# A quantised decoder layer on one Trainium2 core: two running maxima instead of three, joined exponent factors, token halves, and more unread TensorE products

## What is computed

```python
# block 1: fq_* scale by a power of two from the global absolute maximum, round to 8 bits
h    = layer_norm(x) * fq_round(gamma) + fq_round(beta)
qkv  = fq_floor(fq_floor(h) @ fq_round(w_qkv))          # 16 heads of 64
dots = fq_floor(einsum(q, k) * temp)
attn = fq_floor(softmax(dots))
x1   = layer_norm(x + fq_floor(fq_floor(attn @ v) @ fq_round(w_out)))
# block 2: linear cross attention with a 8x8 matrix for each of 16 heads
x2   = layer_norm(x1 + layer_norm(q(x1) @ (k(ctx).T @ v(ctx)) * scale + x1))
# block 3: both products on affine 8-bit codes from the global min and max
out  = layer_norm(x2 + qlinear(gelu(qlinear(x2, W1, b1)), W2, b2))
```

## Time and profile before

| | |
|---|---|
| median of 3 runs | 462.2 us (461.14 to 462.81) |
| profiled execution, its own time | 462.34 us |
| its span, first to last instruction | 460.6 us |
| busy share of the span: DVE, ACT, PE, PEld, POOL | 88%, 75%, 58%, 27%, 31% |
| mean granted TensorE clock | 0.732 of full speed |
| HBM traffic | 7.75 MB read, 1.58 MB written |

### The profile page before, as it was taken

The page is one execution under the profiler, slowest core; times in us unless marked ns, Lnnn a source line. Parts: engine busy times, 40 slices in busy tenths (PEclk is TensorE's granted clock), DMA queues, the critical chain, the costliest instruction groups (busy, mean ns, idle before and its releaser), DMA issues.

```text
span 460.6 us, 7277 instructions
## 1 busy us (share of the span) xinstructions
PE 267.8 (58%) x1800; PEld 126.0 (27%) x1807; DVE 406.2 (88%) x1293; ACT 345.9 (75%) x789; POOL 144.8 (31%) x321
## 2 busy tenths in 40 slices
PE   5688986876677733333323333179997767164371
PEld 3564432332222210000000000033343655051260
DVE  5868998879699999999999999858977986987977
ACT  2599966788999946999999999926676845537233
POOL 2400000001000001999999999970000004530010
PEclk9989997989655555555555555569999997679596
DMA  7600000000444421799899998790002200000002
GB/s 269 160 1 1 1 0 1 24 23 24 176 165 179 186 110 50 161 202 200 200 201 201 204 208 183 137 212 18 1 0 73 85 1 0 1 0 1 0 1 92
DMA packets 84249, 43.24 MB, mean 94 GB/s; under 512 B 69095, under 2 KB 74487, under 8 KB 84090
## 3 DMA queue, kind: packets, MB, share of 16 engines
q1 hardware_dynamic: 82650, 42.69, 36.6%
q10 hardware_dynamic: 1568, 0.21, 0.3%
HBM read 7.75 MB, written 1.58 MB: 20 GB/s over the span
## 4 chain that ended last, share of the span: by engine, by line
DVE 36%; ACT 27%; PE 19%; issue 15%; ACTq 2%; DMA 1%; DVEq 0%; SPq 0%
ACT mem L968 20%; PE ps L471 18%; DVE mem L1090 6%; DVE mem L1250 4%; DVE d_max L1093 4%; DVE mem L1513 3%; DVE m L1650 2%; ACT mem L902 2%; DVE m L1651 2%; ACT mem L938 1%; ACTq L968 1%; DMA mem<-in_x 1%; DVE c L1089 1%; DVE mem L1301 1%; DVE mem L1520 1%
## 5 line engine op out<-in xcount | busy, mean ns | idle before, releaser
L471 PE MATMUL ps<-mem 64*128 64x256 bf16 (+5 forms) x1182 | 179.2, 352 | 113.9 <-DVE row_max L1342 80.0
L968 ACT ACTIVATE mem<-mem,neg_max 128x256 f32<-128x256 int16 x256 | 125.8, 494 | 9.2 <-DVE neg_max L1089 9.2
L471 PEld LDWEIGHTS ps<-mem 64*128 64x128 bf16 (+3 forms) x1188 | 66.2, 118 | 219.0 <-DVE row_max L1342 108.5
L1342 DVE CUSTOM_DVE_ANT_0 mem<-ps,fold,c 128x256 int16<-128x256 f32 x256 | 110.8, 470 | 0.2 <-DVE fold L1090 0.2
L429 POOL TENSOR_SCALAR mem<-mem,r_now 128x256 int16<-128x256 f32 x176 | 81.4, 482 | 76.9 <-DVE r_now L1089 76.8
L471 PE MATMUL ps<-minus,ones_bf 128*128 128x256 bf16 x266 | 38.6, 314 | 32.5 <-DVE m L1651 9.8
L1250 DVE TENSOR_TENSOR mem<-mem 128x1024 bf16<-128x1024 bf16 x76 | 49.7, 685 | 6.3 <-ACT mem L902 3.7
L918 ACT ACTIVATE mem<-ps,c 128x1024 bf16<-128x1024 f32 x48 | 48.3, 1296 | 1.6 <-PE ps L471 1.6
L968 ACT ACTIVATION_READ_ACCUMULATOR mem<-mem,neg_max x256 | 48.3, 189 | 0.0
L938 ACT ACTIVATE mem<-ps,c 128x1024 int16<-128x1024 f32 x32 | 36.2, 1209 | 11.6 <-DVEq L1285 6.2
L471 PEld LDWEIGHTS ps<-minus,ones_bf 128*128 128x128 bf16 x266 | 29.6, 113 | 40.7 <-DVE m L1651 10.2
(11 more groups left out here) (205 smaller groups left out, 358.6 us busy)
## 6 DMA issues: line engine op xcount, KB each, us to landing
...
```

Of the source, the lines that this page charges most:

```text
L471: return te.matmul(o_, l_, r_, start=start, stop=stop)
L968: ins = sc.activation(e_ring[:, u % 4, pos], y_ring[:, u % 4, pos], ACT.Exp, scale=scale_reg, bias=neg_max[:, u % 4, pos:pos + 1], accum_o ...
L1342: ins = ve.tensor_tensor_reduce(y_ring[:, slot, pos], ps[:, 2 * slot + pos // 2, (pos % 2) * N:(pos % 2 + 1) * N], shift, col("g_dots"), - ...
```

## The change

It does the following.

- `max_pass`: two running maxima instead of three. A fold now waits for the fold two back, not three back. After the loop they are joined; then halves of 512 columns are folded onto each other, for the running maximum and for the last unit, so that the last reduction reads 512 columns. The direct maxima (`md`) go onto the diagonal by themselves, and the rest is joined into the diagonal in `across_bf`.
- `scale_of` can give the codes' factor itself: numerators (`numerator`) are made ahead of time. Floors of the dots' shift (`f_qt`) are made in `temperature`, four linked operations there instead of a maximum and a reciprocal after the crossing.
- Behind the attention's product: one maximum over 1024 columns instead of two over 512, joined by the diagonal.
- x2's first rounding moves from DVE to ACT (two halves); both copies of the transposed x2 are DVE's. The hidden units come in the order of `HID_UNITS`; the codes of the hidden layer are made in two halves of tokens, and the second product of a half starts when its four codes are there. `zero_point` comes after the first part of it.
- PE: transposes and products of the cross attention alternate by quarter. `keep_clock` counts change (24 to 36, 24 to 26, 60 to 78, 22 to 32, 40 to 26), new ones are put in (22 before the crossing of the QKV maximum, 18 before the attention's product, 8 after the first transpose of x1), and one product stands ahead of each unit of the QKV code pass but the first three and units 9, 11, 21 and 24. The crossing of the QKV maximum comes ahead of `kv_main(0)` and `kv_bias(0)`.

In the diff, eight leading blanks and unchanged lines are left out; the number is the line before.

```diff
@@ -124 @@
-run_max = at(168, [3, UNIT], BF16)
+run_max = at(168, [2, UNIT], BF16)
@@ -188 @@
+ident_g = diag[:, 1]
@@ -253 @@
+HID_UNITS = [(2 * k + j, h) for k in range(HC // 2) for h in range(2) for j in range(2)]
@@ -459 @@
-    pl.tensor_scalar(hid_i[:, 2], hid[:, 2], col("inv"), 0.0, ALU.mult, ALU.add)\
-        .then_inc(sem("hid_i_pool"), 1)
+    for h in range(2):
+        cols = slice(h * UNIT, (h + 1) * UNIT)
+        pl.tensor_scalar(hid_i[:, 2, cols], hid[:, 2, cols], col("inv"), 0.0, ALU.mult, ALU.add)\
+            .then_inc(sem("hid_i_pool"), 1)
@@ -510 @@
-    keep_clock(24, 6)
+    keep_clock(36, 6)
@@ -633 @@
+            if n >= QKV_RING and n not in (9, 11, 21, 24):
+                keep_clock(1, 2 * (u % QKV_RING))
...
+                keep_clock(22, 6)
+                across_bf(7)
...
-                across_bf(7)
@@ -695 @@
-    keep_clock(24, 1)
+    keep_clock(26, 1)
...
+    keep_clock(18, 1)
@@ -751 @@
-    keep_clock(60, 5)
+    keep_clock(78, 5)
@@ -773 @@
-    for q in range(3):
+    transpose_x1(0)
+    keep_clock(8, 5)
+    for q in range(1, 4):
...
-    for q in range(3):
-        cross_attention(q)
-    transpose_x1(3)
+        cross_attention(q - 1)
@@ -791 @@
-    for u in range(2 * HC):
-        hc, h = u // 2, u % 2
-        if u < 2:
-            pe.wait_ge(sem("x2T_act" if h else "x2T_dve"), 1)
+    for u, (hc, h) in enumerate(HID_UNITS):
+        pe.wait_ge(sem("x2T"), h + 1)
...
-    pe.wait_ge(sem("x2_m"), 10)
-    keep_clock(22, 2)
+    pe.wait_ge(sem("gelu_done"), 2 * HC)
+    pe.wait_ge(sem("x2_m"), 9)
+    keep_clock(32, 2)
...
-    keep_clock(40, 2)
-    pe.wait_ge(sem("hid_codes"), HC)
+    keep_clock(26, 2)
...
+        pe.wait_ge(sem("hid_codes"), HC * (1 + t // 8))
@@ -899 @@
-                sc.activation(run_max[:, nth] if nth < 3 else abs_t[:, nth % 3],
+                sc.activation(run_max[:, nth] if nth < 2 else abs_t[:, nth % 3],
@@ -915 @@
-                sc.activation(run_max[:, k] if first and k < 3 else abs_t[:, k % 3],
+                sc.activation(run_max[:, k] if first and k < 2 else abs_t[:, k % 3],
@@ -981 @@
-            act.wait_ge(sem("o_last"), 2)
+            act.wait_ge(sem("o_last"), 1)
@@ -1052 @@
-    act.wait_ge(sem("x2T_ps"), 2)
-    sc.activation(x2T[:, UNIT:], ps[:, 7].bitcast(BF16), ACT.Copy).then_inc(sem("x2T_act"), 1)
+    act.wait_ge(sem("x2_inv"), 1)
+    for h in range(2):
+        sc.activation(x2_i[:, 8 * h:8 * h + 8], x2[:, 8 * h:8 * h + 8], ACT.Copy,
+                      scale=col("inv")).then_inc(sem("x2_i"), 1)
...
-    for u in range(2 * HC):
-        hc, h = u // 2, u % 2
+    for u, (hc, h) in enumerate(HID_UNITS):
@@ -1064 @@
-    for hc in (1, 3):
-        sc.activation(hid_i[:, hc], hid[:, hc], ACT.Copy, scale=col("inv")).then_inc(sem("hid_i_act"), 1)
+    for h in range(2):
+        for hc in (1, 3):
+            cols = slice(h * UNIT, (h + 1) * UNIT)
+            sc.activation(hid_i[:, hc, cols], hid[:, hc, cols], ACT.Copy, scale=col("inv"))\
+                .then_inc(sem("hid_i_act"), 1)
@@ -1104 @@
-    def across_bf(bank):
-        ts(diag_b[:, 0], ident_b[:], col("m"), None, ALU.mult).then_inc(sem("diagonals"), 1)
+    def across_bf(bank, value, spread):
+        ve.scalar_tensor_tensor(diag_b[:, 0], spread, value, diag_b[:, 0], ALU.mult, ALU.max)\
+            .then_inc(sem("diagonals"), 1)
@@ -1119 @@
-    def scale_of(grown, n, s_out, inv_out, factor=HALF_RANGE, done=None):
+    def scale_of(grown, n, s_out, inv_out, factor=HALF_RANGE, over=float(0x7F000000), done=None):
...
-        ins = ts(inv_out.bitcast(I32), bits, -1.0, float(0x7F000000), ALU.mult, ALU.add)
+        ins = ts(inv_out.bitcast(I32), bits, -1.0, over, ALU.mult, ALU.add)
...
+    def numerator(name):
+        ts(col("n_" + name), col(name).bitcast(I32), float(0x3F800000), None, ALU.add)
+        return ts(col("k_" + name), col(name), HALF_RANGE, None, ALU.mult)
@@ -1205 @@
-    ts(col("k_hw"), col("s_hw"), HALF_RANGE, None, ALU.mult)
+    numerator("s_hw")
@@ -1218 @@
+        link(ts(col("s_qt"), col("s_qq"), col("temp"), None, ALU.mult))
+        link(ts(col("f_qt"), col("s_qt"), 1.0e-30, None, ALU.max))
+        link(ve.reciprocal(col("f_qt"), col("f_qt")))
+        link(ts(col("f_qt"), col("f_qt"), FLOOR, None, ALU.mult))
@@ -1225 @@
-        dve.sem_inc(sem(f"{phase}_folded"), 6)
+        dve.sem_inc(sem(f"{phase}_folded"), 5)
@@ -1243 @@
-                k = nth % 3
-                if 3 <= nth < total - 1:
+                if 2 <= nth < total - 1:
+                    run = run_max[:, nth % 2]
...
-                    dve.wait_ge(sem(f"{phase}_folded"), nth + 1)
-                    ve.tensor_tensor(run_max[:, k], run_max[:, k], abs_t[:, k], ALU.max)\
+                    dve.wait_ge(sem(f"{phase}_folded"), nth + 2)
+                    ve.tensor_tensor(run, run, abs_t[:, nth % 3], ALU.max)\
...
-        k = (total - 1) % 3
-        others = [j for j in range(3) if j != k]
+        half = UNIT // 2
+        run, last = run_max[:, 0], abs_t[:, (total - 1) % 3]
...
-        for j in others:
-            link(ve.tensor_tensor(run_max[:, k], run_max[:, k], run_max[:, j], ALU.max))
+        link(ve.tensor_tensor(run, run, run_max[:, 1], ALU.max))
...
-        link(ts(cb[:, 0:1], col("md"), grow, None, ALU.mult))
+        link(ve.tensor_tensor(run[:, 0:half], run[:, 0:half], run[:, half:], ALU.max))
+        link(ts(diag_b[:, 0], ident_b[:], col("md"), grow, ALU.mult, ALU.mult))
...
-        link(ve.tensor_tensor(run_max[:, k], run_max[:, k], abs_t[:, k], ALU.max))
-        link(ve.tensor_reduce(col("m"), run_max[:, k], AX.X, ALU.max))
-        link(ts(col("m"), cb[:, 0:1], col("m"), None, ALU.max))
+        link(ve.tensor_tensor(last[:, 0:half], last[:, 0:half], last[:, half:], ALU.max))
+        link(ve.tensor_tensor(run[:, 0:half], run[:, 0:half], last[:, 0:half], ALU.max))
+        link(ve.tensor_reduce(col("m"), run[:, 0:half], AX.X, ALU.max))
...
-    across_bf(7)
-    scale_of(col("x"), 1, col("s_qkv"), col("i_qkv"), factor=col("k_hw"))
-    ts(col("g_qkv"), col("s_hw"), col("i_qkv"), None, ALU.mult).then_inc(sem("qkv_scale"), 1)
+    across_bf(7, col("m"), ident_b[:])
+    scale_of(col("x"), 1, col("s_qkv"), col("g_qkv"), factor=col("k_s_hw"), over=col("n_s_hw"), done="qkv_scale")
...
-    dve.wait_ge(sem("qkv_scale"), 1)
@@ -1321 @@
-    across_bf(7)
+    across_bf(7, col("m"), ident_b[:])
...
-    link(ts(col("g_dots"), col("s_qq"), col("temp"), col("i_dots"), ALU.mult, ALU.mult))
+    link(ts(col("g_dots"), col("i_dots"), col("s_qt"), None, ALU.mult))
...
-    dve.wait_ge(sem("dots_scale"), 1)
-    link(ts(col("shift"), col("g_dots"), 1.0e-30, None, ALU.max))
-    link(ve.reciprocal(col("shift"), col("shift")))
...
-        ins = ts(shift[:, k * P:(k + 1) * P], ones[:], col("shift"), FLOOR, ALU.mult, ALU.mult)
+        ins = ts(shift[:, k * P:(k + 1) * P], ones[:], col("f_qt"), col("s_dots"), ALU.mult, ALU.mult)
@@ -1396 @@
-    scale_of(col("x"), 1, col("s_attn"), col("i_attn"))
-    ts(col("g_fine"), col("i_attn"), 1.0 / FINE, None, ALU.mult).then_inc(sem("attn_scale"), 1)
+    scale_of(col("x"), 1, col("s_attn"), col("g_fine"), over=float(0x7F000000 - (14 << 23)), done="attn_scale")
...
-    ts(col("k_av"), col("s_av"), HALF_RANGE, None, ALU.mult)
-    dve.wait_ge(sem("attn_scale"), 1)
+    numerator("s_av")
@@ -1429 @@
+        if grp == 21:
+            link(ts(ident_g, ident[:], GROW, None, ALU.mult))
@@ -1458 @@
+    link(ts(diag_b[:, 0], ident_b[:], col("m"), None, ALU.mult))
...
-    for k in range(2):
-        dve.wait_ge(sem("av_group"), B * GROUPS - 1 + k)
-        absmax(d_max[:, k:k + 1], ps[:, last_bank + k, :]).then_inc(sem("o_last"), 1)
-    dve.wait_ge(sem("o_last"), 2)
-    link(ts(cb[:, 0:1], d_max[:, 0:1], d_max[:, 1:2], GROW, ALU.max, ALU.mult))
-    link(ts(col("m"), cb[:, 0:1], col("m"), None, ALU.max))
-    across_bf(6)
-    scale_of(col("x"), 1, col("s_o"), col("i_o"), factor=col("k_av"))
-    ts(col("g_o"), col("s_av"), col("i_o"), None, ALU.mult).then_inc(sem("o_scale"), 1)
+    dve.wait_ge(sem("av_group"), B * GROUPS)
+    absmax(d_max[:, 0:1], ps[:, last_bank:last_bank + 2].rearrange("p a n -> p (a n)"))\
+        .then_inc(sem("o_last"), 1)
+    dve.wait_ge(sem("o_last"), 1)
+    across_bf(6, d_max[:, 0:1], ident_g)
+    scale_of(col("x"), 1, col("s_o"), col("g_o"), factor=col("k_s_av"), over=col("n_s_av"), done="o_scale")
...
-    ts(col("k_ow"), col("s_ow"), HALF_RANGE, None, ALU.mult)
-    dve.wait_ge(sem("o_scale"), 1)
+    link(numerator("s_ow"))
@@ -1496 @@
-    scale_of(col("x"), 1, col("s_proj"), col("i_proj"), factor=col("k_ow"))
-    ts(col("g_proj"), col("s_ow"), col("i_proj"), None, ALU.mult).then_inc(sem("proj_scale"), 1)
-    dve.wait_ge(sem("proj_scale"), 1)
+    scale_of(col("x"), 1, col("s_proj"), col("g_proj"), factor=col("k_s_ow"), over=col("n_s_ow"), done="proj_scale")
@@ -1629 @@
+    def zero_point():
@@ -1637 @@
+    zero_point()
...
```

(38 more changed lines are left out.)

## The result

The changed kernel takes 454.3 us in the median of four runs (453.64 to 456.63), the kernel before 461.7 us beside it (460.41 to 462.81): ratio 0.9853, 95% interval 0.9824 to 0.9882. The profiled execution takes 454.38 us by its own time, 8.0 less than the one of before; its span is 452.7 us, its mean granted clock 0.749 (0.732 before). The forecast was 452.3 us: 454.3 lies just above its own range (449.5 to 454) and inside the one with the rivals (449.3 to 456.2).

What follows compares the result with a forecast made beforehand. The prediction took the chain of waits to be mostly ACT and DVE, with TensorE on it where its clock is low. Terms summing to 10.05 us off 462.3 gave 452.3 us, own range 449.5 to 454, with rivals 449.3 to 456.2.

Steps and rivals of the forecast that it cites:

- the second rival: POOL takes more of the layer norm's gain and of the hidden codes': 454.3 us, chance 0.14.
- step 1: Join of the maxima, done twice: narrower folds and reduction gain 0.8 us a time, between 0 and 1.6.
- step 9: Start of the kernel: 12 more products may hold the clock over a pause, -0.2 us.
- step 2: QKV code pass: start -0.2, its slow pieces -0.7, half clock -1.3, single products +0.2; -2.0 us, bounds -0.2 and -3.0.
- step 3: Dots: join 0.8, maximum and reciprocal gone behind the crossing 0.4; -1.2 us, bounds -0.4 and -2.0.
- steps 4 and 5: Attention product without half-clock steps, -2.2 us; scale of the product and of the projection, -0.65 us.
- step 6: Layer norm 1 and cross attention: first product and statistics earlier, less POOL contention; -1.7 us, bounds -0.6 and -2.7.
- step 7: Codes of x2: ACT rounds both halves, no longer copies transposed x2, Gelu earlier; -1.2 us, bounds -0.6 and -1.4.
- step 8: Codes of the hidden layer: made in halves, `output(0)` starts at once; -0.9 us, bounds +0.3 and -1.5.
- The first: Rival: the clock still falls in the QKV code pass, 2.0 us lost and about 1.5 more; 455.8 us, chance 0.18.
- The third: Rival: the clock falls between crossing and attention product, 2.2 us lost, up to 1.7 of delay; 456.2 us, chance 0.10.
- the fourth and the fifth: Rivals: added products hold the clock nowhere, 457.5 us, chance 0.04; whole code pass at half clock, 468 us, chance 0.04.

Runs made afterwards that it cites:

- the best version: Changed kernel without code-pass single products, POOL's second hidden half-unit on ACT, 26 products behind x2's crossing, products ahead of code units 3 to 5: 452.4 us, ratio 0.9794.
- the second trace of before: The kernel before, unchanged, run once more for another trace: 462.8 us, one run.

## Why the prediction was right, and where it was not

Direction and cause of most of the gain were right. Four stretches brought 2.3 us less than forecast, three 0.24 more. The sum of 452.3 us missed by 2.0; that 454.3 is also what the second rival had in time is chance, since only a part of the miss was POOL's.

**Join (step 1).** Right: 0.76 against 0.8 a time, shown by putting it back.

**Start (step 9), 0.2 forecast, 0.20 measured.** This is not shown to be a gain: eleven traces with the same instructions up to there reach the last maximum at 64.42 to 64.97 us, and the two of before at 64.71 and 64.46.

**QKV code pass (step 2), 2.0 forecast, 1.07 measured.** The forecast was 0.2 for the start, 0.7 for its slow pieces, 1.3 for the fall at 101 us, less 0.2 for the single products. Set against the best version's trace, which has no single products and full clock throughout, the terms measure 0.02, 0.51 (first to fourth unit 8.16 us before, 7.65 there), 1.44 and, for the products, 0.85. So three things failed. DVE's start gained nothing: from the last maximum to its first unit it is 8.98 us before and 8.96 after, since what `temperature` and the longer diagonal add takes up all that join and factor save. "Two of them show, +0.2" put the products' cost at a quarter: PE is the chain in more places than at `xm_half` (38.96 us against 38.11, both at full clock). Its premise, a DVE step of 2.2 us throughout, was read from the last units only; in the changed kernel seven of the fifteen steps are longer than 2.4 us. And "in the 5.18 us piece half clock costs 1.3" was right as a size in that trace (6.24 us against 4.80 for the two steps of DVE) but no effect of the change: it was one execution's, since the second trace of before lacks it, and so does the changed kernel without any products. That the products hold the clock in this pass is not shown by any run.

**Dots (step 3), 1.2 forecast, 0.77 measured.** The exponentials' first row maxima came 1.12 us earlier against the last maximum, as forecast; 0.35 was lost again just ahead of the row sums' minimum, where DVE idles before an operation of 128x8:

```profile
300.26 0.20 DVE L1369 RECIPROCAL row_inv<-row_sums 128x8 f32<-128x8 f32 x1 [3.37 <-ACT mem L975]
300.92 0.17 DVE L1101 TENSOR_SCALAR r_now<-row_inv 128x8 f32<-128x8 f32 x1 [0.46 <-DVE row_inv L1369]
```

Before, the second starts 0.31 us behind the first. The run with the old join has 0.31 too, with the same instructions there, and so has the second trace of before; all eleven traces with the new join have 0.66. So it is no matter of one execution. Of the 0.77 us that the new join saves at the dots about 0.3 reach this minimum (138.59 us with the old join, 138.26 here). What the idle time is stays open.

**Attention product and scales (steps 4 and 5), 2.85 forecast, 2.95 measured.** Right in sum, with luck in it: taking the products away gives back 1.4, not 2.2, and the second trace of before is 0.8 quicker in this stretch than the first, by which the gain would be 2.2. So my steps at half clock were counted rightly, but from a trace that had more of them.

**Cross attention (step 6), 1.7 forecast, 1.84 measured.** The sum was right and its reason wrong. I gave the gain to the order and called the 78 products a means to it. The runs gave 0.1 to the order, since DVE's wait for POOL takes back what it saves, and 1.7 to the products and with them the clock. Both halves of that had stood in the prediction: three transposes at half clock, and up to two shifts losing 0.5.

**Codes of x2 (step 7), 1.2 forecast, 0.67 measured.** The term of the first unit was mis-sized: in this execution the clock fell as the hidden layer's first products began (0.83 in 409 to 410 us, 0.50 after), and Gelu waited 0.43 us for them. In the traces where the clock is up the stretch takes 7.34 to 7.36 us, which would be 1.1.

**Hidden codes (step 8), 0.9 forecast, 0.46 measured.** `output(0)` did start at once. The mis-sized term is POOL's: the codes, from the reciprocal's end on, took 6.94 us against 6.17, 0.77 longer, where I had put 0.34, because DVE's clamps stretched beside POOL's second half; shown by taking that half away. And PE, at 0.50 in 437 to 440 us, kept the second read waiting for 0.39 us. That wait is of this execution: four traces with the same instructions there lack it and take 41.3 us up to the end, which would be a gain of 0.96.

**The rivals.** The first, a clock that still falls in the code pass, was wrong for the changed kernel's trace and true in its condition for three of the five traces that have its instructions there (0.58, 0.57 and 0.79 in 74 to 78 us); their units took 0.3 to 0.7 us more, not the 3.5 of its price. The second, POOL taking more, named the right place for a third of what was missing. The third, a fall ahead of the attention product, did not come while its 18 products stood; neither did the fourth and the fifth.

**The signs.** The clock was 1.00 from 66 to 116 us, the attention product stepped by 0.66 from its start, DVE idled 0.99 us before its first statistics, and the last stage's first read did not wait. Three signs came out wrong. The steps between code units were up to 3.61 us. The exponentials' first ACT row came 2.4 us earlier (176.75 to 174.35), not 3, since the code pass gave less. And one of DVE's shifts took 1.24 us beside POOL's `x2_b2`; the kernel before had one of 1.23.
